# A graph, attention and expert kernel on one core: variance batches, fillers and three small steps in another order

## The chip, the cores and the metric

The kernel runs on one core of a Trainium2 chip. The metric is the device time of one execution in microseconds (us), all work included. The engines are named as in the profile: PE is TensorE's matrix product, PEld its weight load, ACT is ScalarE, DVE is VectorE, POOL is GpSimd, SP is SyncE, which issues the transfers.

## The reference

Three parts follow each other. First a graph network over 50 joints of 4096 frames: three layers of attention over a chain of joints (each joint sees itself and its two neighbours), each with a layer norm over the features and a GELU.

```python
h = _gat(x, src, dst, W, a_s, a_d, bg)      # softmax over neighbours, 4 heads
res = x @ R
x = jax.nn.gelu(_layer_norm(h + res, g, b), approximate=False)
...
x = x.reshape(Bb * Tt, J * DIMS[-1]) @ fpW + fpb
x = _layer_norm(x, fng, fnb)
```

The widths are 3, 64, 128 and 64. The result, one token of 128 numbers per frame, is set beside a text of 128 tokens. Then comes a memory attention (query projection, a causal convolution over 4 steps, a normalised query through two small matrices) and a mixture of 8 experts of width 512, of which each token takes the two best:

```python
h = jnp.concatenate([h, txt], axis=1)
h = h + _L0_attn_ref(_layernorm(h, axis=-1), ...)
h = h + _L0_ffn_ref(_layernorm(h, axis=-1), ...)
```

## The kernel before

The work goes in 16 rounds (`STEPS`). A round takes 256 frames, as two groups of 128 (`GH = 2`), through the three graph layers, and in the gaps it does the attention and the experts of the round before. Everything stays in SBUF, only the inputs of a round, its text and its output move by DMA. Each engine has its own program, written out by hand as one function per step (`window`, `iteration`, `graph_layer` and so on under `block.tensor`, `block.scalar`, `block.vector`, `block.gpsimd`, `block.sync`), and it runs in exactly that order; the engines meet through counting semaphores.

*Tasks.* The joints are taken in chunks of four (13 chunks, the last with two joints). Layer 1 has 26 tasks (chunk and group), layer 2 has 13 (both groups side by side), layer 0 has 14 tasks of its own shape (`task0`, the last two with 128 columns, the others with 512). A task holds up to 512 columns, one PSUM bank.

*Layer 0* (in `window`). PE computes a task's own product (`own_0`, L780) into one of four banks. ACT copies it to SBUF (`take_0`, L1393) and squares every odd task from the bank (L1397); POOL squares the even ones from the copy (`squares_0`, L551). The squares lie in a ring of six (`SQ`, `SQN = 6`), and PE sums them over the features in batches of four tasks (`variance`, L768). A product waits until its bank is free, that is for ACT's copy (even tasks) or square (odd tasks) of the task four before. A square of task 6 or later waits until the batch that read its place in the ring is done. Between them PE runs fillers (`keep_warm`, L684): products of constants whose result nobody reads. Behind the last batch ACT copies the sums (`variance_out`, L1402), PE turns them (`variance_rows`, L788), DVE computes the inverse deviation (`rstd`, from L2112 on, `rsqrt` L2034 to L2041, and its split into bf16 parts L2117 to L2120), PE turns it back (`rstd_rows`, L795), ACT copies it (L1407), PE spreads it over the partitions (`spread_rstd`, L808 and L812) and DVE multiplies (`normalise`, L2138).

*Layers 1 and 2* (`graph_layer` on PE and ACT, `neighbours` on DVE). For each task PE spreads the attention weights (L923, L926), computes the neighbour's product (L906, L909), which ACT copies (`take_d`), and the own product (L944, L948). DVE in layer 2 forms differences of joints (`joint_differences`, L2064 to L2076), scales both neighbours in one operation (L2099), then adds the own product and the neighbour ahead (L2106). POOL subtracts the neighbour behind:

```python
TT(dst, dst, TQ[:, k % 3, 0:cols], ALU.subtract).then_inc(zs_ok, 1)   # take_behind, L580
```

ACT squares the result (`square`, L1484), and PE sums the squares in batches of four tasks; layer 1 has seven batches, layer 2 has four. At the end of a layer PE also starts an expert of the round before: `up(s - 1, e, (0,))` and `(1,)` are two of the four units of an expert's first product (L1043), `down` its second product (L1052). They stand around the last two batches:

```python
if tail:
    pe.wait_ge(d_sb, s * AGG + T0[l] - NT0 + NT[l])
    up(s - 1, e, (0,))
variance(s, l, BATCHES[l] - 2)
if tail:
    pe.wait_ge(t_ok, s * AGG + T0[l] - NT0 + NT[l] + 1)
    up(s - 1, e, (1,))
variance(s, l, BATCHES[l] - 1)
```

The wait for `t_ok` is one for DVE's last scaling, whose banks the unit reuses. ACT's activation of the first unit (`hidden`, L1539) waits for the batch before the last, since it overwrites a place of the ring, and stands ahead of the last square.

*DVE beside the layers.* Behind layer 1's tasks stands the choice of each token's two experts (`top_two`, L2244 to L2270), then `rstd`. Ahead of layer 2's tasks stand the additions of experts (`add_expert`, L2281) and the two sums of the next round's softmax of layer 0 (`alphas(..., (0,))`, L1826 and L1829); its other parts (L1835, L1837) stand behind tasks 2, 5 and 8. Behind layer 2's tasks stand the coordinates of the next round (`coordinates`, from L1885 on), then `rstd`.

Of the kernel before, what the change touches and what calls it, by code (L numbers as in the profile page):

```python
# [10 lines left out]
P = 128  # L11
# [52 lines left out]
def build(nc, A, out):  # L64
# [3 lines left out]
    with ctx:  # L68
# [417 lines left out]
        def _(pool):  # L486
# [87 lines left out]
            def take_behind(s, l, n):  # L574

                c, gh = task(l, n)
                k, cols, o = T0[l] - NT0 + n, joints(c) * P, c * NCOL
                pool.wait_ge(zt_ok, s * AGG + k + 1)
                dst = X2[:, gh, o:o + cols] if l == 1 else X1[:, o:o + cols]
                TT(dst, dst, TQ[:, k % 3, 0:cols], ALU.subtract).then_inc(zs_ok, 1)  # L580

            def layer_1(s):

                mean_differences(s, 1)
                pool.wait_ge(parts_ok, s * 2 + 1)
                pool.wait_ge(x_ok, s * NPAIR + PAIRS[0])
                difference_1(s, 0)
                difference_1(s, 1)
                for n in range(NT[1]):
                    if n % GH == 0 and n // GH + 2 < NCH:  # L590
                        difference_1(s, n // GH + 2)
                    take_behind(s, 1, n)

            def query_pads(s):

# [9 lines left out]
            def iteration(s, nxt):  # L605
                layer_1(s)
                if nxt:
                    pool.wait_ge(r_ps, s * NPAIR + P0[1] + 1)
                    scores_0(s + 1)
                    edges_0(s + 1)  # L610
                mean_differences(s, 2)
                for n in range(NT[2]):
                    take_behind(s, 2, n)
                    if nxt and n == 9:
                        pose_pads(s + 1)
                query_pads(s)
                if nxt:
                    squares_0(s + 1)
# [26 lines left out]
        def _(pe):  # L645
# [338 lines left out]
            def graph_layer(s, l, tail, moe):  # L984

                e = 0 if l == 1 else 4
                if l == 1:
                    product_d(s, l, 0)
                alphas_ready(s, l)
                for n in range(NT[l]):  # L990
                    if l == 2 and n == 1 and tail:
                        added(s - 1, 3)
                    early = l == 2 and n > 0
                    if early and n + 1 < NT[l]:
                        product_d(s, l, n + 1)
                    spread_alpha(s, l, n)
                    if not early and n + 1 < NT[l]:
                        product_d(s, l, n + 1)
                    if n == 0:
                        mean_rows(s, l)  # L1000
                        if l == 1 and moe:
                            added(s - 2, 7)
                    own(s, l, n, True)
                    minus_mean(s, l, n)
                    if l == 1 and n == 5 and tail:
                        token_columns(s - 1, bank[5])
                    if l == 1 and n == 7 and tail:
                        token_logits(s - 1)
                    if l == 1 and n == 9 and tail:
                        pe.wait_ge(lgm_ok, s)  # L1010
                        variance(s, l, 0)
                    elif n % 4 == 3 and n >= 7 and not (n == 7 and l == 1 and tail):
                        variance(s, l, n // 4 - 1)
                if tail:
                    pe.wait_ge(d_sb, s * AGG + T0[l] - NT0 + NT[l])
                    up(s - 1, e, (0,))
                variance(s, l, BATCHES[l] - 2)
                if tail:
                    pe.wait_ge(t_ok, s * AGG + T0[l] - NT0 + NT[l] + 1)
                    up(s - 1, e, (1,))  # L1020
                variance(s, l, BATCHES[l] - 1)
                if tail:
                    pe.wait_ge(hid_sb, (s - 1) * E * MT + e * MT + 2)
# [13 lines left out]
            def up(t, e, units=range(MT)):  # L1037

                for m in units:
                    k = e * MT + m  # L1040
                    if m >= 2 or e == 7:
                        pe.wait_ge(hid_sb, t * E * MT + k)
                    mm(hidden_bank(e, m), w1[:, k * P:k * P + P], XT2[:], start=True, stop=True).then_inc(hid_ps, 1)  # L1043
# [41 lines left out]
            def window(w, main, tail, moe):  # L1085

                t = w - 1
                if main:
                    pe.wait_ge(yt_sb, w * 4 + 4)
                    for n in range(NT0):  # L1090
                        if n == 2 and tail:
                            pe.wait_ge(hf_ok, t + 1)
                        own_0(w, n)
                        if n in (3, 7):
                            keep_warm(3, bank[0])
                        if n % 4 == 1 and n >= 5:
                            keep_warm(2 if n == 5 else 5, bank[0])
                            variance(w, 0, n // 4 - 1)
                    variance(w, 0, BATCHES[0] - 1)
                    if moe:  # L1100
                        up(t - 1, 5, (0,))
                    variance_rows(w, 0)
# [604 lines left out]
        def _(dve):  # L1707
# [371 lines left out]
            def neighbours(s, l, n):  # L2079
# [20 lines left out]
                if l == 2 and n + 1 < NT[l]:  # L2100
# [5 lines left out]
                STT(dst, bZ[(NT0 + k) % 2][:, 0:cols], bgc[:, l - 1:l], TQ[:, 3, 0:cols], ALU.add, ALU.add)\  # L2106
                    .then_inc(zt_ok, 1)

            def rstd(s, l):

                dve.wait_ge(vt_ps, s * 3 + l + 1)
                link(TS(VB.rearrange("p (q a n) -> p q a n", q=CJ, a=4),  # L2112
                        bank[0].rearrange("p (q a n) -> p q a n", q=CJ, a=4)[:, :, :, 0:VR // 4], EPS, None, ALU.add))
                rsqrt(RV, VB, RN)

                vp, rp = (x.rearrange("p (q n) -> p q n", q=CJ) for x in (VB, RV))
                link(nc.vector.tensor_copy(RG[:, :, 0, :], rp))  # L2117
                link(TT(vp, rp, RG[:, :, 0, :], ALU.subtract))
                link(nc.vector.tensor_copy(RG[:, :, 1, :], vp))
                TT(RG[:, :, 2, :], vp, RG[:, :, 1, :], ALU.subtract).then_inc(rg_ok, 1)  # L2120
                dve.wait_ge(zs_ok, s * TASKS + T0[l] + NT[l])
# [221 lines left out]
            def iteration(s, moe, nxt):  # L2343

                t = s - 1
                for n in range(NT[1]):
                    neighbours(s, 1, n)
                    if moe and n == 7:
                        logits(t)
                if moe:  # L2350
                    for part in range(6):
                        top_two(t, part)
# [15 lines left out]
                if moe:  # L2368
                    add_bias(t)
                    add_expert(t, 2)  # L2370
                    add_expert(t, 3)
                if nxt:
                    alphas(s + 1, 0, F0b, M0, Al0, (0,))
                for n in range(NT[2]):
                    neighbours(s, 2, n)
                    if nxt and n in (2, 5, 8):
                        alphas(s + 1, 0, F0b, M0, Al0, ({2: 3, 5: 4, 8: 2}[n],))
                if nxt:
                    coordinates(s + 1, 0)
                rstd(s, 2)  # L2380
# [162 lines left out]
```

## Time and profile before

| what | value |
|---|---|
| median of 3 runs | 4307.02 us (4305.0 to 4308.09) |
| the profiled execution, own time | 4305.8 us |
| its span, first to last instruction | 4304.0 us |
| PE busy | 3816.6 us (89%) |
| DVE busy | 3451.0 us (80%) |
| ACT busy | 2351.6 us (55%) |
| POOL busy | 1507.9 us (35%) |
| granted clock of TensorE, mean | 0.974 of full |
| HBM read and written | 14.72 MB and 4.19 MB |

How to read it: all rows of the trace come from one execution, so a sum over them is set against 4305.8 us. The shares of busy time are means over stages with different limits. The granted clock is 1.00 at 2.4 GHz and 0.50 at 1.2 GHz; a stretch between these had some of each. In a timeline a row may merge several instructions of one kind; the arrow in brackets names who ended an idle time. A product of fp32 operands shows as two instructions in the trace.

### The profile page before, as it was taken

How to read it: one execution, taken by the hardware profiler on the slowest of the kernel's cores; microseconds unless marked ns; L12 is line 12 of the kernel's file. 1: busy time of each engine (PE TensorE's matmuls, PEld its weight loads, DVE VectorE, ACT ScalarE, POOL GpSimd, SP SyncE). 2: the span in 40 equal slices, each digit the busy share in tenths (PEclk: the TensorE clock that was granted, in tenths of full speed). 3: DMA queues.
4: the chain of work that ended last, by engine and by line, in shares of the span. 5: the costliest groups of instructions: out<-in, count | busy, mean ns of one | idle time of the engine just before them, and what ended most of it. 6: DMA issues, size and time to landing. Idle time of an engine off the chain costs nothing.

```text
span 4304.0 us, 61949 instructions
## 1 busy us (share of the span) xinstructions
PE 3816.6 (89%) x22762; PEld 1767.0 (41%) x22762; DVE 3451.0 (80%) x6559; ACT 2351.6 (55%) x3833; POOL 1507.9 (35%) x1513
## 2 busy tenths in 40 slices
PE   4888889898988989889898989989899898988988
PEld 2232344334434344353433434343354343434345
DVE  3878878788787888878788787888878788787872
ACT  2545556465655646556465665646556455664643
POOL 2624315252342524315243341624315243242410
PEclk8898999999999999999999999999999999999999
DMA  2000000000000000000000000000000000000000
GB/s 96 1 4 1 1 6 1 4 3 2 5 1 4 3 4 3 1 6 1 4 3 2 5 1 4 3 4 3 1 6 1 4 3 2 5 1 4 4 2 6
DMA packets 22816, 22.97 MB, mean 5 GB/s; under 512 B 3378, under 2 KB 21818, under 8 KB 22122
## 3 DMA queue, kind: packets, MB, share of 16 engines
q1 hardware_dynamic: 22506, 18.93, 1.4%
q8 instruction: 183, 3.00, 0.3%
q14 instruction: 127, 1.04, 0.1%
HBM read 14.72 MB, written 4.19 MB: 4 GB/s over the span
## 4 chain that ended last, share of the span: by engine, by line
PE 46%; DVE 35%; ACT 10%; issue 7%; POOL 1%; DVEq 0%; SPq 0%; DMA 0%; ACTq 0%; POOLq 0%
DVE R L2099 8%; PE bank L906 7%; PE bank L1043 6%; PE bank L1052 5%; PE bank L768 4%; DVE X L2106 4%; PE bank L840 3%; ACT X L1413 2%; DVE X L2138 2%; DVE R L1831 2%; PE bank L780 2%; PE bank L923 2%; PE bank L909 2%; PE bank L829 2%; DVE R L2073 2%
## 5 line engine op out<-in xcount | busy, mean ns | idle before, releaser
L580 POOL TENSOR_TENSOR X<-X,R 128x512 f32<-128x512 f32 (+1 forms) x624 | 787.4, 1262 | 819.8 <-DVE X L2106 815.8
L2099 DVE TENSOR_TENSOR R<-bank,R 128x1024 f32<-128x1024 f32 (+1 forms) x624 | 738.8, 1184 | 74.5 <-PE bank L923 2.1
L2138 DVE TENSOR_TENSOR X<-X,bank 128x1024 f32<-128x1024 f32 (+2 forms) x432 | 484.7, 1138 | 250.6 <-PE bank L808 125.1
L1413 ACT ACTIVATE X<-X,c_vec 128x1024 f32<-128x1024 f32 (+2 forms) x432 | 498.2, 1173 | 218.3 <-DVE X L2138 215.2
L1043 PE MATMUL bank<-XT,c_w 128*128 128x512 f32 x1024 | 524.1, 627 | 15.4 <-DVE Ho L2281 7.8
L1052 PEld LDWEIGHTS bank<-c_w,SQ 128*128 128x128 f32 x4096 | 489.2, 192 | 90.8 <-issue 84.0
L1052 PE MATMUL bank<-c_w,SQ 128*128 128x128 f32 x4096 | 513.0, 278 | 0.0
L906 PE MATMUL bank<-R,c_W 64*128 64x512 f32 (+1 forms) x832 | 464.7, 639 | 34.1 <-ACT R L1456 18.8
L2106 DVE SCALAR_TENSOR_TENSOR X<-bank,bgc,R 128x512 f32<-128x512 f32 (+1 forms) x624 | 455.9, 731 | 28.4 <-PE bank L960 6.2
L1539 ACT ACTIVATE SQ<-bank,c_vec 128x512 f32<-128x512 f32 x512 | 346.4, 686 | 225.6 <-PE bank L1043 175.2
L944 PE MATMUL bank<-X,WR 64*128 64x512 f32 (+1 forms) x832 | 463.7, 638 | 2.8 <-DVE Ho L2281 2.8
L1454 ACT ACTIVATE R<-bank 128x512 f32<-128x512 f32 (+1 forms) x416 | 241.3, 580 | 376.2 <-PE bank L906 290.5
L1484 ACT ACTIVATE SQ<-X 128x512 f32<-128x512 f32 (+1 forms) x624 | 375.2, 609 | 108.7 <-POOL X L580 102.3
L560 POOL TENSOR_TENSOR Al<-R 128x208 f32<-128x208 f32 x128 | 87.2, 710 | 916.1 <-ACT R L1380 916.1
L1461 ACT ACTIVATE R<-bank 128x512 f32<-128x512 f32 (+1 forms) x208 | 121.4, 584 | 377.9 <-PE bank L910 320.7
L569 POOL TENSOR_TENSOR R<-X 128x512 f32<-128x512 f32 (+1 forms) x208 | 268.2, 1292 | 151.2 <-DVE Pt L1846 95.0
L551 POOL TENSOR_TENSOR SQ<-X 128x512 f32<-128x512 f32 (+1 forms) x112 | 106.6, 952 | 578.8 <-ACT X L1393 577.1
L1043 PEld LDWEIGHTS bank<-XT,c_w 128*128 128x128 f32 x1024 | 176.3, 193 | 256.5 <-issue 129.4
L948 PE MATMUL bank<-X,WR 128*64 128x512 f32 (+1 forms) x832 | 215.0, 594 | 52.5 <-DVE X L2106 50.7
L923 PE MATMUL bank<-AT,sel1b 120*128 120x512 bf16 (+1 forms) x832 | 250.2, 383 | 8.4 <-DVE R L2099 6.7
L910 PE MATMUL bank<-X,c_W 128*64 128x512 f32 (+1 forms) x416 | 217.0, 603 | 0.0
L909 PE MATMUL bank<-X,c_W 128*64 128x512 f32 (+1 forms) x416 | 217.0, 603 | 0.0
(288 smaller groups left out, 6250.0 us busy)
## 6 DMA issues: line engine op xcount, KB each, us to landing
c_w<-in_w SPq DMA_DIRECT2D x2, 2048.0 KB
out<-Ho SPq DMA_DIRECT2D x32, 128.0 KB, 1.9
c_fpW<-in_fpW SPq DMA_DIRECT2D x1, 3200.0 KB
X<-in_x SPq DMA_DIRECT2D x34, 75.0 KB, 2.0
X<-in_txt SPq DMA_DIRECT2D x32, 64.0 KB, 1.9
X<-in_sel SPq DMA_DIRECT2D x1, 600.0 KB
X<-in_sel SPq DMA_DIRECT2D x1, 300.0 KB
X<-in_raw SPq DMA_DIRECT2D x1, 256.0 KB
```

Source lines behind the costliest of these rows:

```text
L580: TT(dst, dst, TQ[:, k % 3, 0:cols], ALU.subtract).then_inc(zs_ok, 1)
L906: mm(bD[:, 0:cols], W1[64 * gh:64 * gh + 64, :], DX[64 * gh:64 * gh + 64, c % 2, 0:cols], start=True, stop=True).then_inc(d_ps, 1)
L923: last = mm(b[:, 0:cols], sel1[:, c % JS, :], AT[:, sign, gh, o:o + cols], start=True, stop=True)
L944: mm(z[:, 0:cols], WR1[64 * gh:64 * gh + 64, :], X1[64 * gh:64 * gh + 64, o:o + cols], start=True, stop=False)
L1043: mm(hidden_bank(e, m), w1[:, k * P:k * P + P], XT2[:], start=True, stop=True).then_inc(hid_ps, 1)
L1052: last = mm(b[:, q * P:q * P + P], HD[:, m, q * P:q * P + P], w2[:, k * P:k * P + P], start=(m == 0 and q == 0), stop=(m == MT - 1), skip_ ...
L1413: A_(dst, dst, ACT.Gelu, bias=v(f"b{l}"), scale=v(f"g{l}")).then_inc(x_ok, 1)
L1484: A_(SQ[:, n % SQN, 0:cols], z, ACT.Square).then_inc(sq_ok, 1)
L1539: A_(HD[:, m, :], hidden_bank(e, m), ACT.Gelu, bias=vec[:, FB1 + k:FB1 + k + 1]).then_inc(hid_sb, 1)
L2099: TT(TQ[:, k % 3:4:3 - k % 3, 0:cols], bR[k % 2][:, :, 0:cols], both, ALU.mult).then_inc(t_ok, 1)
L2106: STT(dst, bZ[(NT0 + k) % 2][:, 0:cols], bgc[:, l - 1:l], TQ[:, 3, 0:cols], ALU.add, ALU.add)\
L2138: TT(dst, dst, b, ALU.mult).then_inc(u_ok, 1)
```

## The change

In every place it is the order that changes, and in one the engine.

- Layer 0 in `window` on PE: the variance batch of tasks 0 to 3 now follows product 7 (before: product 5), that of 4 to 7 follows product 11 (before: 9), that of 8 to 11 follows product 13 as before, and that of the last two tasks is last. Of fillers there are four behind product 3, three ahead of each of the last two batches: ten. Before there were 3, 2, 3, 5 and 5: eighteen.
- The subtraction of the last chunk (`take_behind`) moves from POOL to DVE: two tasks of 256 columns in layer 1, one in layer 2. DVE waits there for POOL's subtraction of the task before.
- In layer 2 the expert unit `up(s - 1, e, (1,))` and its wait stand ahead of the third variance batch.
- On DVE the two sums `alphas(s + 1, 0, ..., (0,))` stand behind task 0 of layer 2 instead of ahead of it.

```diff
@@ gpsimd, layer_1
-                    take_behind(s, 1, n)
+                    if n // GH + 1 < NCH:
+                        take_behind(s, 1, n)
@@ gpsimd, iteration
-                for n in range(NT[2]):
+                for n in range(NT[2] - 1):
                     take_behind(s, 2, n)
@@ tensor, graph_layer
-                variance(s, l, BATCHES[l] - 2)
+                if l == 1:
+                    variance(s, l, BATCHES[l] - 2)
                 if tail:
                     pe.wait_ge(t_ok, s * AGG + T0[l] - NT0 + NT[l] + 1)
                     up(s - 1, e, (1,))
+                if l == 2:
+                    variance(s, l, BATCHES[l] - 2)
                 variance(s, l, BATCHES[l] - 1)
@@ tensor, window
                         own_0(w, n)
-                        if n in (3, 7):
-                            keep_warm(3, bank[0])
-                        if n % 4 == 1 and n >= 5:
-                            keep_warm(2 if n == 5 else 5, bank[0])
+                        if n == 3:
+                            keep_warm(4, bank[0])
+                        if n % 4 == 3 and n >= 7:
                             variance(w, 0, n // 4 - 1)
-                    variance(w, 0, BATCHES[0] - 1)
+                    for i in range(NT0 // 4 - 1, BATCHES[0]):
+                        keep_warm(3, bank[0])
+                        variance(w, 0, i)
@@ vector
+            def take_behind(s, l, n):
+
+                c, gh = task(l, n)
+                k, cols, o = T0[l] - NT0 + n, joints(c) * P, c * NCOL
+                dve.wait_ge(zt_ok, s * AGG + k + 1)
+                dve.wait_ge(zs_ok, s * TASKS + NT0 + k)
+                dst = X2[:, gh, o:o + cols] if l == 1 else X1[:, o:o + cols]
+                TT(dst, dst, TQ[:, k % 3, 0:cols], ALU.subtract).then_inc(zs_ok, 1)
@@ vector, iteration
                     if moe and n == 7:
                         logits(t)
+                take_behind(s, 1, NT[1] - 2)
+                take_behind(s, 1, NT[1] - 1)
...
-                if nxt:
-                    alphas(s + 1, 0, F0b, M0, Al0, (0,))
                 for n in range(NT[2]):
                     neighbours(s, 2, n)
+                    if nxt and n == 0:
+                        alphas(s + 1, 0, F0b, M0, Al0, (0,))
                     if nxt and n in (2, 5, 8):
                         alphas(s + 1, 0, F0b, M0, Al0, ({2: 3, 5: 4, 8: 2}[n],))
+                take_behind(s, 2, NT[2] - 1)
```

The instructions of PE in layer 0 of a round in the middle, before (L780 own products, L684 fillers, L768 variance batches; a count is in instructions of the program):

```order
L780 MATMUL bank<-X,W0bd 128x512 x4
L684 MATMUL bank<-sel1b 128x512 x3
L780 MATMUL bank<-X,W0bd 128x512 x2
L684 MATMUL bank<-sel1b 128x512 x2
L768 MATMUL bank<-SQ,V2p 32x512 x4
L780 MATMUL bank<-X,W0bd 128x512 x2
L684 MATMUL bank<-sel1b 128x512 x3
L780 MATMUL bank<-X,W0bd 128x512 x2
L684 MATMUL bank<-sel1b 128x512 x5
L768 MATMUL bank<-SQ,V2p 32x512 x4
```

The same place in the changed kernel, where the three kinds are L781, L685 and L769:

```order
L781 MATMUL bank<-X,W0bd 128x512 x4
L685 MATMUL bank<-sel1b 128x512 x4
L781 MATMUL bank<-X,W0bd 128x512 x4
L769 MATMUL bank<-SQ,V2p 32x512 x4
L781 MATMUL bank<-X,W0bd 128x512 x4
L769 MATMUL bank<-SQ,V2p 32x512 x4
L781 MATMUL bank<-X,W0bd 128x128 x2
L685 MATMUL bank<-sel1b 128x512 x3
L769 MATMUL bank<-SQ,V2p 32x512 x4
L685 MATMUL bank<-sel1b 128x512 x3
L769 MATMUL bank<-SQ,V2p 32x128 x2
```

Four products now stand in a row ahead of each of the first two batches, and no filler is between them.

The instructions of DVE at the start of layer 2, before (L1826 and L1829 are the two sums, L2099 the scaling, L2106 the addition of a task):

```order
L2281 SCALAR_TENSOR_TENSOR Ho<-bank,router,Ho 128x128 x8
L1826 TENSOR_TENSOR X<-X 128x416
L1829 TENSOR_TENSOR X<-X 128x416
L2064 MEMSET R 128x128
L2073 TENSOR_TENSOR R<-R 128x512
L2099 TENSOR_TENSOR R<-bank,R 128x1024
L2071 TENSOR_TENSOR R<-R 128x128
L2073 TENSOR_TENSOR R<-R 128x512
L2106 SCALAR_TENSOR_TENSOR X<-bank,bgc,R 128x512
L2099 TENSOR_TENSOR R<-bank,R 128x2x512
```

And in the changed kernel (the sums are L1831 and L1834, the scaling is L2104, the addition L2111):

```order
L2295 SCALAR_TENSOR_TENSOR Ho<-bank,router,Ho 128x128 x8
L2069 MEMSET R 128x128
L2078 TENSOR_TENSOR R<-R 128x512
L2104 TENSOR_TENSOR R<-bank,R 128x1024
L2076 TENSOR_TENSOR R<-R 128x128
L2078 TENSOR_TENSOR R<-R 128x512
L2111 SCALAR_TENSOR_TENSOR X<-bank,bgc,R 128x512
L1831 TENSOR_TENSOR X<-X 128x416
L1834 TENSOR_TENSOR X<-X 128x416
L2104 TENSOR_TENSOR R<-bank,R 128x2x512
```

The two sums have moved from ahead of the first differences to between the addition of task 0 and the scaling of task 1.

## Rows read from the trace of the kernel before

**Rows 1.** The page, its first line.

```profile
span 4304.0 us, 61949 instructions
```

**Rows 2.** Timeline, layer 0 (start us, us, engine, line, operation, count, idle before).

```profile
2125.17 0.82 PE L684 MATMUL bank<-sel1b 120*128 120x512 bf16 x3
...
2126.28 1.11 ACT L1393 ACTIVATE X<-bank 128x512 f32<-128x512 f32 x2
...
2127.24 0.65 ACT L1397 ACTIVATE SQ<-bank 128x512 f32<-128x512 f32 x1
...
2128.07 1.06 PE L768 MATMUL bank<-SQ,V2p 128*32 128x512 f32 x8
...
2128.45 1.06 POOL L551 TENSOR_TENSOR SQ<-X 128x512 f32<-128x512 f32 x1 [0.43 <-ACT X L1393]
...
2129.07 1.13 PE L780 MATMUL bank<-X,W0bd 32*128 32x512 f32 x4
...
2131.94 1.25 PE L684 MATMUL bank<-sel1b 120*128 120x512 bf16 x5
...
2138.24 1.12 PE L1043 MATMUL bank<-XT,c_w 128*128 128x512 f32 x2
```

**Rows 3.** Timeline, start of layer 2 in the same round.

```profile
2048.90 0.58 DVE L1826 TENSOR_TENSOR X<-X 128x416 f32<-128x416 f32 x1
...
2052.85 0.29 DVE L2071 TENSOR_TENSOR R<-R 128x128 f32<-128x128 f32 x1 [0.68 <-ACT R L1461]
...
2053.78 0.75 DVE L2106 SCALAR_TENSOR_TENSOR X<-bank,bgc,R 128x512 f32<-128x512 f32 x1
...
2054.61 1.28 POOL L580 TENSOR_TENSOR X<-X,R 128x512 f32<-128x512 f32 x1 [17.75 <-DVE X L2106]
2054.66 1.23 DVE L2099 TENSOR_TENSOR R<-bank,R 128x1024 f32<-128x1024 f32 x1
```

**Rows 4.** Busy time of DVE by stretch, layer 2's loop (us, busy, clock, DMA).

```profile
2053.80:2091.80 38.00, 35.83 (x50) 1.00 0.02 4
```

**Rows 5.** Timeline, end of layer 2, same round; last the view of L1886 (ns).

```profile
2090.50 2.54 POOL L580 TENSOR_TENSOR X<-X,R 128x512 f32<-128x512 f32 x2 [1.28 <-DVE X L2106]
...
2091.28 0.48 DVE L2106 SCALAR_TENSOR_TENSOR X<-bank,bgc,R 128x256 f32<-128x256 f32 x1
...
2092.38 1.31 DVE L1886 TENSOR_TENSOR X<-Al,dX 128x600 f32<-128x600 f32 x1
...
2092.49 1.45 PE L768 MATMUL bank<-SQ,V2p 128*32 128x512 f32 x8 [2.62 <-ACT SQ L1484]
...
2093.86 2.07 PE L1043 MATMUL bank<-XT,c_w 128*128 128x512 f32 x2
...
2098.27 0.29 DVE L2112 TENSOR_SCALAR R<-bank 128x128 f32<-128x128 f32 x1 [2.30 <-PE bank L788]
...
L1886 DVE TENSOR_TENSOR X<-Al,dX x32: 774/778/1312, 54.0 to 3914.8; 128x600 f32<-128x600 f32 x32
```

**Rows 6.** Timeline, end of layer 2 one round later.

```profile
2349.31 0.48 DVE L2106 SCALAR_TENSOR_TENSOR X<-bank,bgc,R 128x256 f32<-128x256 f32 x1
...
2354.87 0.29 DVE L2112 TENSOR_SCALAR R<-bank 128x128 f32<-128x128 f32 x1 [0.87 <-PE bank L788]
```

**Rows 7.** PE by stretch at ends of layer 2 (us, busy, clock, DMA, GB/s).

```profile
1053.00:1061.00 8.00, 5.92 (x20) 0.79 0.00 0
...
4155.00:4163.00 8.00, 4.95 (x17) 0.79 0.04 10
```

**Rows 8.** Timeline, end of layer 1; last the view of L2246 (ns min/median/max).

```profile
2251.16 0.29 DVE L2112 TENSOR_SCALAR R<-bank 128x128 f32<-128x128 f32 x1
...
2255.22 0.42 PE L795 MATMUL bank<-identb,R 128*96 128x128 bf16 x4 [1.49 <-DVE R L2120]
...
L2246 DVE TENSOR_TENSOR router<-router,den x16: 191/520/523, 437.9 to 4234.7; 128x32 f32<-128x32 f32 x16
```

**Rows 9.** Timeline, a DVE product of two tensors with 256 columns.

```profile
2118.45 0.42 DVE L2138 TENSOR_TENSOR X<-X,bank 128x256 f32<-128x256 f32 x1 [2.02 <-PE bank L812]
```

## The prediction

> **What bounds the kernel now.** I read the page first, then the order of the program, then the timeline of one round of the 16 (2040 to 2300 us), then the granted clock. The span is 4304.0 us [rows 1]; the profiled execution took 4305.8 us, 1.2 us under the median 4307.02 us. No engine is the bound all through, so each edit is priced in its own stage. Four places matter.
>
> *Layer 0's own products.* TensorE (PE) runs in program order: products, fillers, a variance batch. The reader is to see that ScalarE (ACT) waits for PE here: two copies take 1.11 us and a square 0.65 us [rows 2], and they overlap, so that a pair costs some 1.43 us and seven pairs under 10 us, while the stage lasts from 2125.17 (after the first four products) to 2138.24, 13.07 us. VectorE (DVE) is on the path only behind it.
>
> *Layer 2's loop.* DVE is busy 35.83 of 38.00 us [rows 4] over 50 operations; the rest is the short gap between dependent ones. Whatever is added there moves the end. Ahead of it, between the first scaling and 2052.85, DVE waits 0.68 us for ACT [rows 3].
>
> *The end of layer 2.* PE sits idle some 2.6 us before the third variance batch; then its clock falls to the lower level. The batch takes 1.45 us, the expert unit behind it 2.07 us, and DVE starts the inverse deviation at 2098.27, 6.99 us after its last addition began (2091.28) [rows 5]. In a round whose clock stays up that stretch is 5.56 us (2349.31 to 2354.87) [rows 6]. Of 15 rounds with an expert, 11 show a mean clock below 1.00 there, the first and the last of them in [rows 7].
>
> *The end of layer 1.* The router's top-two work on DVE ends just when the transposed variances are there: L2112 starts at 2251.16 with no wait shown [rows 8]. It has no slack, and PE waits for DVE behind it.
>
> **The change part by part.** Times are of the same round; 26.14 stands for 2126.14 in layer 0, 91.3 for 2091.3 in layer 2.
>
> *(a) Layer 0: eight fillers fewer, variances later.* A filler costs 0.215 us ((1.25 − 0.82)/2 of 5 and 3), a batch 1.00 us until the next product starts (28.07 to 29.07), a pair of products 1.06 us with what it waits for [rows 2]. Walking the new order: four fillers 25.17 to 26.03, product 4 at 26.14; 5 waits for the square of 1, behind which ACT's copies start at 26.28, so 26.4; 6 starts at 26.87 behind the copy of 2, 7 at 27.94 behind the square of 3 (27.24 + 0.65); batch 0 at 29.0, 8 to 10 at 30.0, 11 at 30.8 behind the square of 7, batch 1 at 31.86, the two small products at 32.86, three fillers to 33.85. Batch 2 waits for GpSimd's (POOL's) square of task 10 (1.06 us, [rows 2]) until 34.3; three fillers, batch 3 to about 36.3. Before: 38.24. That is 1.9 us a round. Bounds: eight fillers alone are 1.7 us; ACT's pace allows 3. Behind it lies a chain of PE, ACT and DVE that starts with the variances, so all of it counts: 16 x 1.9 = **−30 us**.
>
> *(b) Expert unit ahead of layer 2's third batch.* Unit 1 moves into PE's idle stretch: it needs only DVE's last scaling, done when the last addition starts (91.28), so it runs from 91.3 to 92.4, and the gap of 2.6 us becomes one of 1.4. If that keeps the clock, a round saves what the two kinds differ by, 6.99 − 5.56 = 1.43 us, in 11 rounds. In every round it saves little more: behind batch 2 ACT still has an expert activation and the last square, and batch 3 waits for them anyway; some 0.2 us. 11 x 1.43 + 15 x 0.2 = **−19 us**. Bounds: −3 (the clock falls all the same) and −25 (1.65 us in all 15).
>
> *(c) The last subtractions on DVE.* One of 256 columns costs about 0.42 us [rows 9]. In layer 2 it is hidden: POOL's own one (part of 2.54 us) goes, and with it the delay of the next product of the coordinates, 1.31 us instead of the usual 0.78 [rows 5]; DVE stays ahead of the variances: nothing. In layer 1 two of them (0.87 us with their waits) stand ahead of the top-two work, which has no slack. A part comes back: L2246 takes 0.52 us in the median and 0.19 alone [rows 8], since POOL's subtraction ran beside it, and that is gone: +0.55 us. ACT's squares gain nothing, since the activation between them waits for a batch. 15 x 0.55 = **+8 us**. Bounds 0 and +13.
>
> *(d) Layer 0's two sums for the softmax behind the first task of layer 2.* Before, they ran from 48.90 on, the first for 0.58 us [rows 3], ahead of the loop; without them DVE would have waited longer for ACT's copy at 52.85, so they were free. Now they stand behind the addition of task 0 (53.78 + 0.75 [rows 3]) in the saturated loop. Alone the two cost 1.2 us and a short gap, less what they overlap with the addition's end and the wait that they fill: +1.05 us. But POOL starts its subtraction of that task at 54.61 [rows 3]. At the end of layer 2 the same meeting is seen: L1886, second of two DVE multiplications of two SBUF tensors with a POOL subtraction pending, takes 1.31 for 0.78 us [rows 5]; POOL went in between the two. Here POOL would take its 1.1 to 1.3 us between the two sums: the second ends at about 56.6 and the next scaling moves from 54.66 to 56.66, +2.0 us. Bounds +1.05 and +2.2; I take 2.0, since L1886 is the same situation. 15 x 2.0 = **+30 us**.
>
> The Trainium skill speaks against this edit: "SBUF — State Buffer", section "Who interferes with whom", says that a DVE instruction with two SBUF inputs and a GpSimd instruction that reads SBUF lock each other out for a whole instruction. By it the second sum waits for all of POOL's subtraction, the upper end; the trace agrees where it shows it (1.31 against 0.78 us).
>
> *(e) The clock in new gaps.* With (c) PE's gap at the end of layer 1 grows from 1.49 [rows 8] to 2.0 us, with two expert steps of 2 us behind it that would run at half clock. Gaps of 2.6 us behind thin work gave a fall in 11 of 15 rounds; I count a fall here in 6 of 15, at 1.4 us (the price at layer 2): +8. For (a), where PE now runs some 3 us with small products only, and for what is left at layer 2, another +5. Sum **+13 us**; bounds 0 and +35.
>
> Sum: −30 − 19 + 8 + 30 + 13 = +2, against the execution's own 4305.8 us 4307.8 us, and with the 1.2 us between it and the median 4309 us. A measurement of this kernel can tell about 0.2% (8.6 us) from no change, so this is "no change".
>
> **The rivals.**
> 1. *The clock holds everywhere.* (e) is nothing: 4309 − 13 = 4296 us, faster. For it: gaps of 1.5 us at layer 1 never cost the clock. Against it: the gaps grow towards what did.
> 2. *The two sums are cheap.* POOL does not get in between: (d) is 1.05 x 15 = 16 instead of 30: 4295 us, faster. With rival 1 as well: 4282 us. Against it: L1886.
> 3. *The clock falls in more places* (slower): at layer 1's end in every round. Nine more falls of 1.4 us give 4322 us. It decides if the 2.0 us gap works as the 2.6 us one did; its price is the expert steps behind the gap. For it: all gaps of 2.6 us but four fell.
> 4. *The moved expert unit does not keep the clock* (the change does not do there what it is for): (b) is −3 instead of −19: 4325 us. Against it: the gap nearly halves, and the unit fills its end.
>
> **How the numbers follow.** Forecast 0.42, with its own range 4299 to 4315. Rivals 1 and 2 together 0.30, rival 3 0.17, rival 4 0.11. The time is the likeliest case's, 4309 us. The range reaches into rivals 1 and 2 (4287) and over 3 and 4 (4327), which leaves out the double cases. Faster by over 0.2% (under 4298.4 us) 0.30, within it 0.42, slower (over 4315.6) 0.28.
>
> **What would show each step.** (a) ACT's last copy of layer 0 followed by the expert product 1.9 us earlier relative to the first fillers, granted clock 1.00 in the stage. (b) The stretch from DVE's last addition to L2112's successor at about 5.4 us in all rounds, the unit in front of the batch. (c) The same stretch in layer 1 up by 0.5 us, the router's product at 0.19 us. (d) The second sum at over 1 us with POOL's subtraction inside it, and the next scaling 2 us later than before, relative to the first. (e) Falls of the clock behind layer 1's end in about 6 rounds. The prediction is wrong if (d) costs 1 us or less or if layer 0 saves under 1.5 us, and if the falls are fewer than 3 or more than 12.

## The result and the profile after

The changed kernel takes 4312.70 us in the median of 20 runs (4305.62 to 4317.94), the kernel before 4304.74 us in 20 runs of the same series (4296.97 to 4310.08): a ratio of 1.0020 with the interval 1.0013 to 1.0027. The forecast was 4309 us, 2 us over the kernel before; the measured difference is 8.0 us. The sign is measurable, the size stands right at the 0.2% that the prediction called no change.

The page of the changed kernel, its first two lines and the granted clock, against [rows 1]:

```profile
span 4307.5 us, 61756 instructions
...
PE 3799.3 (88%) x22634; PEld 1769.5 (41%) x22634; DVE 3487.7 (81%) x6607; ACT 2349.2 (55%) x3833; POOL 1465.4 (34%) x1465
...
PEclk8999999999999999999999999999999999999999
```

The profiled execution took 4309.3 us, 3.4 us under the median. Its span is 3.5 us longer than before's. The page shows nothing else, since the edits cancel each other. To see them, each round is cut on DVE's timeline at the points that bound its stages, from the start of one pose token (the step that closes a round) to the start of the next. The table gives means over the 15 full rounds in us, and the difference times 15. It is worked out from the timelines of both kernels. A stretch begins and ends where the operations named in it start; the inverse deviation starts at L2112 (L2126 in the changed kernel).

| stretch, from and to | before | after | x15 |
|---|---|---|---|
| pose token to layer 0's inverse deviation | 16.27 | 14.49 | −26.7 |
| first normalised product of layer 0 to first addition of layer 1 (the attention stage) | 45.57 | 45.06 | −7.7 |
| layer 1: last addition to inverse deviation | 4.64 | 5.05 | +6.2 |
| layer 1: inverse deviation to first normalised product | 6.87 | 7.74 | +13.1 |
| layer 2: first addition to next scaling | 0.89 | 2.73 | +27.6 |
| layer 2: last addition to inverse deviation | 6.52 | 5.62 | −13.6 |
| layer 2: inverse deviation to first normalised product | 6.16 | 6.81 | +9.7 |
| the others | 171.27 | 171.21 | −0.9 |
| whole round (sum) | 258.19 | 258.71 | +7.7 |

Ahead of the first pose token 4.3 us are won (313.20 to 308.86 us), which with the +7.7 makes the 3.5 us of the span. In these 4.3 lie the first pass of layer 0, 1.9 us shorter (its inverse deviation starts at 80.03 us for 81.93), and the first pair of sums, 2.0 us longer; the other 4.4 us go with a mean granted clock of 0.88 there for 0.86.

**Layer 0.** The timeline of PE in the changed kernel, for [rows 2] (start us, us, engine, line, operation, operands, count, idle before; L781 own products, L685 fillers, L769 variance batches):

```profile
2124.93 1.04 PE L685 MATMUL bank<-sel1b 120*128 120x512 bf16 x4
...
2125.90 2.92 PE L781 MATMUL bank<-X,W0bd 32*128 32x512 f32 x8
2128.74 1.06 PE L769 MATMUL bank<-SQ,V2p 128*32 128x512 f32 x8
...
2133.10 0.82 PE L685 MATMUL bank<-sel1b 120*128 120x512 bf16 x3
...
2134.14 1.07 PE L769 MATMUL bank<-SQ,V2p 128*32 128x512 f32 x8 [0.21 <-POOL SQ L551]
...
2136.23 1.12 PE L1047 MATMUL bank<-XT,c_w 128*128 128x512 f32 x2
```

From the first of the fillers to the expert product behind the last batch it is 11.30 us; before 13.07 [rows 2]. Batch 2 waits for POOL's square, as the walk said.

**Start of layer 2.** The timeline, for [rows 3]:

```profile
2052.18 0.75 DVE L2111 SCALAR_TENSOR_TENSOR X<-bank,bgc,R 128x512 f32<-128x512 f32 x1
...
2052.85 0.58 DVE L1831 TENSOR_TENSOR X<-X 128x416 f32<-128x416 f32 x1
2053.01 1.55 POOL L580 TENSOR_TENSOR X<-X,R 128x512 f32<-128x512 f32 x1 [17.76 <-DVE X L2111]
2053.47 1.54 DVE L1834 TENSOR_TENSOR X<-X 128x416 f32<-128x416 f32 x1
2055.05 1.23 DVE L2104 TENSOR_TENSOR R<-bank,R 128x1024 f32<-128x1024 f32 x1
```

The scaling starts 2.87 us after the addition, for 0.88 [rows 3]. POOL's subtraction is ready in the middle of the first sum, and goes in ahead of the second, which lasts 1.54 us. It does so in all 15 places behind task 0; the 16th stands ahead of the first round and takes 0.59 us, so that the view by line gives a mean of 1.48 us (busy us, mean ns):

```profile
L1834 DVE TENSOR_TENSOR X<-X 128x416 f32<-128x416 f32 x16 | 23.7, 1484 | 0.6
```

**End of layer 2.** The timeline, for [rows 5]:

```profile
2091.66 0.48 DVE L2111 SCALAR_TENSOR_TENSOR X<-bank,bgc,R 128x256 f32<-128x256 f32 x1
2091.68 1.12 PE L1047 MATMUL bank<-XT,c_w 128*128 128x512 f32 x2 [1.44 <-DVE R L2104]
...
2092.26 0.43 DVE L2121 TENSOR_TENSOR X<-X,R 128x256 f32<-128x256 f32 x1
2092.87 1.06 PE L769 MATMUL bank<-SQ,V2p 128*32 128x512 f32 x8
...
2095.10 0.62 PE L769 MATMUL bank<-SQ,V2p 128*32 128x256 f32 x2 [1.16 <-ACT SQ L1489]
2096.49 0.86 PE L789 MATMUL bank<-c_ident,R 128*128 128x128 f32 x4 [0.78 <-ACT R L1407]
...
2097.15 3.38 PE L1047 MATMUL bank<-XT,c_w 128*128 128x512 f32 x4
2097.46 0.29 DVE L2126 TENSOR_SCALAR R<-bank 128x128 f32<-128x128 f32 x1 [1.10 <-PE bank L789]
...
2102.15 0.39 PE L796 MATMUL bank<-identb,R 128*96 128x128 bf16 x4
...
2104.15 1.22 DVE L2152 TENSOR_TENSOR X<-X,bank 128x1024 f32<-128x1024 f32 x1 [2.67 <-PE bank L813]
```

The batch is at full clock now (1.06 us, for 1.45 [rows 5]) and L2126 starts 5.80 us after the last addition, for 6.99. But the clock falls all the same, some 3 us later: the transposes take 0.86 us and the expert product behind them 3.38 us, so that the transposes of the deviations (L796) come late. Part of what was won is given back. The same two in the kernel before, in the round whose clock holds [rows 6]:

```profile
2354.13 0.63 PE L788 MATMUL bank<-c_ident,R 128*128 128x128 f32 x4 [0.78 <-ACT R L1402]
2354.60 1.88 PE L1043 MATMUL bank<-XT,c_w 128*128 128x512 f32 x4
```

**End of layer 1.** First a round whose clock stays up, for [rows 8]:

```profile
2247.08 0.19 DVE L2260 TENSOR_TENSOR router<-router,den 128x32 f32<-128x32 f32 x1
...
2250.44 0.28 DVE L2126 TENSOR_SCALAR R<-bank 128x128 f32<-128x128 f32 x1
...
2254.50 0.42 PE L796 MATMUL bank<-identb,R 128*96 128x128 bf16 x4 [1.87 <-DVE R L2134]
2254.76 2.00 PE L1056 MATMUL bank<-c_w,SQ 128*128 128x128 f32 x16
...
2257.31 2.35 DVE L2152 TENSOR_TENSOR X<-X,bank 128x1024 f32<-128x1024 f32 x2 [2.86 <-PE bank L809]
```

And the same place in another round of the same execution:

```profile
1474.97 0.42 PE L796 MATMUL bank<-identb,R 128*96 128x128 bf16 x4 [1.87 <-DVE R L2134]
1475.23 3.46 PE L1056 MATMUL bank<-c_w,SQ 128*128 128x128 f32 x16
...
1479.41 2.35 DVE L2152 TENSOR_TENSOR X<-X,bank 128x1024 f32<-128x1024 f32 x2 [4.49 <-PE bank L809]
```

PE's stretches around it (from and to, length, busy, granted clock):

```profile
1471.00:1476.00 5.00, 3.13 (x20) 0.95 0.00 0
1476.00:1480.00 4.00, 4.00 (x21) 0.63 0.00 0
```

The gap of PE is 1.87 us (before 1.49 [rows 8]); in both rounds it is the same. In the second the unit behind it runs at the lower level, 3.46 us for 2.00, and DVE gets its bank 1.64 us later (8.50 for 6.87 us in the table's stretch). That happens in 8 of 15 rounds; before in none.

### The profile page after: what moved, and what is told of

It reads as the page before. It is cut to its first block, busy times and chain, and to the rows that moved or that the text cites. A ratio compares the mean times of both kernels' runs of the same rounds, so it can differ in the third digit from the quotient of the medians.

```text
span 4307.5 us, 61756 instructions
## 1 busy us (share of the span) xinstructions
PE 3799.3 (88%) x22634; PEld 1769.5 (41%) x22634; DVE 3487.7 (81%) x6607; ACT 2349.2 (55%) x3833; POOL 1465.4 (34%) x1465
## 4 chain that ended last, share of the span: by engine, by line
DVE 48%; PE 35%; ACT 9%; issue 6%; POOL 1%; DVEq 1%; SPq 0%; DMA 0%; ACTq 0%; POOLq 0%
DVE R L2104 14%; DVE X L2111 8%; PE bank L1056 6%; PE bank L1047 6%; PE bank L841 3%; PE bank L907 2%; PE bank L781 2%; ACT X L1418 2%; PE bank L769 2%; DVE X L2152 2%; DVE R L1836 2%; DVE R L2078 2%; DVE Ho L2295 2%; PE bank L830 2%; ACT AT L1440 1%
## 5 line engine op out<-in xcount | busy, mean ns | idle before, releaser
L580 POOL TENSOR_TENSOR X<-X,R 128x512 f32<-128x512 f32 x576 | 750.3, 1303 | 829.7 <-DVE X L2111 828.2
L2104 DVE TENSOR_TENSOR R<-bank,R 128x1024 f32<-128x1024 f32 (+1 forms) x624 | 738.7, 1184 | 72.2 <-PE bank L924 1.0
L1047 PE MATMUL bank<-XT,c_w 128*128 128x512 f32 x1024 | 533.4, 638 | 37.1 <-DVE R L2104 21.6
L1056 PEld LDWEIGHTS bank<-c_w,SQ 128*128 128x128 f32 x4096 | 503.2, 196 | 97.5 <-issue 90.7
L1056 PE MATMUL bank<-c_w,SQ 128*128 128x128 f32 x4096 | 525.9, 282 | 0.0
L2111 DVE SCALAR_TENSOR_TENSOR X<-bank,bgc,R 128x512 f32<-128x512 f32 (+1 forms) x624 | 455.9, 731 | 24.5 <-PE bank L961 2.0
L1047 PEld LDWEIGHTS bank<-XT,c_w 128*128 128x128 f32 x1024 | 178.9, 195 | 282.8 <-issue 121.6
```

Of the source, the lines that this page charges most:

```text
L1056: last = mm(b[:, q * P:q * P + P], HD[:, m, q * P:q * P + P], w2[:, k * P:k * P + P], start=(m == 0 and q == 0), stop=(m == MT - 1), skip_ ...
L2104: TT(TQ[:, k % 3:4:3 - k % 3, 0:cols], bR[k % 2][:, :, 0:cols], both, ALU.mult).then_inc(t_ok, 1)
```

## The experiments

Two theories stood against each other. **Sum of the parts:** each edit does what its term says, so that each alone gives its term, and leaving out the costly one gives the rest. **The clock decides:** the parts are right by themselves, but each also shifts where PE's clock falls, so that the parts don't add. Each run's kernel before ran beside it on the same chip (4307.14, 4306.47 and 4306.83 us in three series). Stage times and counts of falls below are of each one's profiled execution, cut as in the table: one execution a kernel, so how they vary between executions was not seen.

**1. Only layer 0's order** (the hunk `@@ tensor, window` of the change alone):

```diff
-                        if n % 4 == 1 and n >= 5:
-                            keep_warm(2 if n == 5 else 5, bank[0])
...
+                        if n % 4 == 3 and n >= 7:
                             variance(w, 0, n // 4 - 1)
...
```

> Layer 0's order alone (four products ahead of a batch, ten fillers), all else as before. Theory A (each term stands by itself): layer 0's stage is 1.8 us a round shorter and everything behind it moves along, 16 rounds, so 27 to 30 us faster than before (ratio 0.993 to 0.994), with the granted clock never falling in that stage. Rival (the gain is given back later, at the attention or the clock): under 15 us faster (ratio above 0.9965).

Measured: 4271.85 us, ratio 0.9920 (0.9907 to 0.9934), so −35, 5 us more than theory A's range. Layer 0 gives 1.78 us a round, −26.7, and 1.9 us in its first pass. Beyond it the attention stage lost 9.6 us of falls and the start 8.3 us (the 1.9 among them), and the end of layer 2 got 10.4 us longer (in 4 rounds 8.11 us, both halves of the stretch at the lower clock). The term holds; what came on top goes with the clock.

**2. Only the two sums:**

```diff
-                if nxt:
-                    alphas(s + 1, 0, F0b, M0, Al0, (0,))
                 for n in range(NT[2]):
                     neighbours(s, 2, n)
+                    if nxt and n == 0:
+                        alphas(s + 1, 0, F0b, M0, Al0, (0,))
```

> Only the two sums of layer 0's softmax moved behind the first task of layer 2. Theory A: DVE's loop is saturated and GpSimd's subtraction gets in between the two sums, so 2.0 us in each of 15 rounds, 28 to 31 us slower (ratio 1.0065 to 1.007). Rival: a part is absorbed by the wait ahead of layer 2's second task, 1.05 us or less a round, at most 16 us slower (ratio 1.004 or less).

Measured: 4338.93 us, ratio 1.0072 (1.0058 to 1.0086), so +32. The next scaling is 1.98 us later in every round whose sums stand there. With layer 0's, this term is what both theories share, and it holds.

**3. The whole change, with the sums back in their old place:**

```diff
+                if nxt:
+                    alphas(s + 1, 0, F0b, M0, Al0, (0,))
                 for n in range(NT[2]):
                     neighbours(s, 2, n)
-                    if nxt and n == 0:
-                        alphas(s + 1, 0, F0b, M0, Al0, (0,))
```

> The changed kernel with the two sums back ahead of the loop (so layer 0's order, the subtractions on DVE and the expert unit). Theory A: the changed kernel less 28 us, so about 4285 us and 20 us faster than before (ratio 0.995). Rival (the parts hide each other): less than 15 us below the changed kernel.

Measured: 4266.99 us, ratio 0.9912 (0.9898 to 0.9925); 46 us under the changed kernel where the sums cost 28. The rest is clock: at the end of layer 1 one fall is left of eight, though the gaps there are alike (1.85 to 2.24 us in the changed kernel, 1.87 to 2.26 us here), and behind the unit in layer 2 none is left of fourteen. That speaks for the second theory: the same gap gave falls or not by what stood elsewhere in the round.

**4. Only the expert unit ahead of the batch:**

```diff
-                variance(s, l, BATCHES[l] - 2)
+                if l == 1:
+                    variance(s, l, BATCHES[l] - 2)
                 if tail:
                     pe.wait_ge(t_ok, s * AGG + T0[l] - NT0 + NT[l] + 1)
                     up(s - 1, e, (1,))
+                if l == 2:
+                    variance(s, l, BATCHES[l] - 2)
```

> Only the expert unit ahead of layer 2's third variance batch. Theory A (from the trace of the changed kernel: the clock no longer falls ahead of the batch but falls behind it in nearly every round, so the stretch to the inverse deviation is 0.9 us shorter and the next one 0.65 us longer): 2 to 6 us faster than before. Rival (the forecast's term): 15 to 20 us faster, ratio 0.996. From the last addition to the inverse deviation about 5.5 us in every round, from there to the first product with it 6.9 us.

Measured: 4297.39 us, ratio 0.9978 (0.9969 to 0.9987), so −10, between the ranges of the two theories: neither was met. The profiled execution was the fastest of its runs, 4289.97, and its start is 7.7 us shorter than before. The stretch to the inverse deviation falls from 6.52 to 5.58 us in the mean (−14.1), the next grows in 9 rounds, for the 14 of the changed kernel, by 0.42 in the mean (+6.3).

**5. Only the subtractions on DVE:**

```diff
+                take_behind(s, 1, NT[1] - 2)
+                take_behind(s, 1, NT[1] - 1)
...
+                take_behind(s, 2, NT[2] - 1)
```

> Only the last subtractions on DVE (two in layer 1, one in layer 2). Theory A: in layer 1 the stretch from the last addition to the inverse deviation grows by 0.42 us a round, in layer 2 it is hidden; 15 x 0.42, about 6 us slower than before (ratio 1.001 to 1.002), plus a fall of the clock behind layer 1 in rounds whose gap lies badly (1.6 us each, 0 to 8 of them). Rival: the shorter delay of the next instruction pays for it, within 2 us of before.

Measured: 4341.25 us, ratio 1.0083 (1.0070 to 1.0097), so +35 where its direct cost (5.08 for 4.64 us) is 6.6. Theory A was missed by far, and this is the best witness of the second theory. Layer 1's end shows a fall in 11 of 15 rounds (+17.1 us), and layer 2's end costs 11.8 us more than before. In six of the eleven rounds layer 2's stretch to the inverse deviation takes 8.10 us; the timeline of such a round:

```profile
2364.11 0.48 DVE L2107 SCALAR_TENSOR_TENSOR X<-bank,bgc,R 128x256 f32<-128x256 f32 x1
...
2365.31 1.93 PE L769 MATMUL bank<-SQ,V2p 128*32 128x512 f32 x8 [2.62 <-ACT SQ L1485]
...
2367.17 2.08 PE L1044 MATMUL bank<-XT,c_w 128*128 128x512 f32 x2
...
2371.02 1.09 PE L789 MATMUL bank<-c_ident,R 128*128 128x128 f32 x4 [0.78 <-ACT R L1403]
...
2372.21 0.29 DVE L2122 TENSOR_SCALAR R<-bank 128x128 f32<-128x128 f32 x1 [3.41 <-PE bank L789]
```

The gap of 2.62 us is that of the kernel before, and the batch behind it at the lower clock from its start, 1.93 us: the whole chain to L2122 then is, and takes 8.10 us instead of 6.99 or 5.56 [rows 5, 6].

**6. The sums split, the first behind task 0, the second behind task 1:**

```diff
-                    link(TT(Mx[:], Mx[:], Fb[:, 2, :], ALU.add))
+                    if 5 not in parts:
+                        link(TT(Mx[:], Mx[:], Fb[:, 2, :], ALU.add))
+                if 6 in parts:
+                    link(TT(Mx[:], Mx[:], Fb[:, 2, :], ALU.add))
...
+                    if nxt and n < 2:
+                        alphas(s + 1, 0, F0b, M0, Al0, ((0, 5) if n == 0 else (6,)))
```

> The kernel before with the two sums in the loop, but one behind task 0 and the other behind task 1 of layer 2, so that GpSimd's subtraction can't stand between them. Theory A (2.0 us a round were 1.05 of length and 0.95 of GpSimd's turn on the way to SBUF): from the first addition to the next scaling 0.45 to 0.6 us longer than before, the same behind task 1, together 1.0 to 1.2 us a round, 15 to 18 us slower than before (ratio 1.0035 to 1.0042). Rival (length and saturation alone, GpSimd plays no part): 2.0 us a round as with both sums together, 28 to 31 us slower (ratio 1.007).

Measured: 4316.11 us, ratio 1.0027 (1.0017 to 1.0037), so +10. The timeline behind task 0:

```profile
2054.34 0.75 DVE L2109 SCALAR_TENSOR_TENSOR X<-bank,bgc,R 128x512 f32<-128x512 f32 x1
2055.01 0.58 DVE L1826 TENSOR_TENSOR X<-X 128x416 f32<-128x416 f32 x1
2055.17 1.56 POOL L580 TENSOR_TENSOR X<-X,R 128x512 f32<-128x512 f32 x1 [17.76 <-DVE X L2109]
2055.63 1.22 DVE L2102 TENSOR_TENSOR R<-bank,R 128x1024 f32<-128x1024 f32 x1
```

With one sum there, the scaling (one operand from the bank, one from SBUF) runs straight through POOL's subtraction, 1.29 us after the addition. Each of the two sums costs 0.40 us, together 0.80 instead of 1.98. Of the difference, 0.95 us is what the second sum of the pair lasted over its own 0.59: the wait for POOL. The time stays under theory A's range of 15 to 18 us. The old place still is better, being free.

**7. The changed kernel with six fillers ahead of layer 1's gap:**

```diff
                     down(t, 0, (0,))
+                    keep_warm(6, bank[3])
```

> The changed kernel with six fillers in TensorE's gap at the end of layer 1, behind the first unit of the expert's second product. Theory A (8 of 15 rounds lost 1.64 us there to the lower clock): the stretch from layer 1's inverse deviation to its first product is 6.87 us in every round again, about 13 us under the changed kernel, 4300 us. Rival (the fillers themselves delay the turned rows): 6.87 us is not reached, or under 5 us gained.

Measured: 4293.63 us, ratio 0.9974 (0.9964 to 0.9984); 19 us under the changed kernel. PE's timeline there:

```profile
2243.35 1.05 PE L1056 MATMUL bank<-c_w,SQ 128*128 128x128 f32 x8
2244.24 1.46 PE L685 MATMUL bank<-sel1b 120*128 120x512 bf16 x6
2246.29 0.42 PE L796 MATMUL bank<-identb,R 128*96 128x128 bf16 x4 [0.58 <-DVE R L2135]
2246.55 2.00 PE L1056 MATMUL bank<-c_w,SQ 128*128 128x128 f32 x16
```

The gap is 0.58 us, L1056 takes 2.00 us, and the stretch is 6.87 us in all 15 rounds: with the gap mostly filled no fall is left at layer 1's end, where they cost 13.1 us. Seven of the fourteen falls in layer 2 went with them, untouched by the fillers.

**8. Layer 0's order and the unit, subtractions and sums as before** (against the changed kernel):

```diff
-                take_behind(s, 1, NT[1] - 2)
-                take_behind(s, 1, NT[1] - 1)
...
+                if nxt:
+                    alphas(s + 1, 0, F0b, M0, Al0, (0,))
```

> Layer 0's order and the expert unit, with the subtractions on GpSimd and the sums ahead of the loop as before. Theory A: the subtractions cost 6 us in the run with the sums back (4267 us), so about 4261 us, 46 us faster than before (ratio 0.989). Rival (what these runs gained beyond their terms was the clock's luck with the length of a round): no faster than 4267 us, for rounds of another length meet more falls.

Measured: 4257.85 us (4256.55 to 4258.93), ratio 0.9889 (0.9874 to 0.9904): 49 us under the kernel before, 55 under the changed one. It beats both. Falls are left in layer 0 (3 rounds, 16.2 for 14.5 us), one at layer 2's end, and 10 in the attention stage of the 14 later rounds (45.7 us and more for 44.8).

**9. Number 8 without the ten fillers of layer 0:**

```diff
-                        if n == 3:
-                            keep_warm(4, bank[0])
...
-                        keep_warm(3, bank[0])
```

> The best so far (layer 0's new order and the expert unit, 4258 us) without any of the ten fillers in layer 0. Theory A (the fillers are there for the clock): TensorE's clock falls in layer 0's stage in half of the rounds or more, the stage from the pose token to the inverse deviation is 16 us or longer there instead of 14.5, and the time is 4265 to 4285 us. Rival (the waits for ScalarE and GpSimd set the pace, the clock holds): the stage is 0.5 to 1 us shorter in every round, 4243 to 4252 us.

Measured: 4315.04 us, ratio 1.0020 (1.0011 to 1.0029), 57 us over number 8 and over what was expected. Layer 0 takes 18.48 us in the mean for 14.83. PE's stretches in one round, the first four products and the rest:

```profile
2129.10:2133.10 4.00, 3.69 (x14) 1.00 0.00 0
2133.10:2147.60 14.50, 13.96 (x52) 0.53 0.00 0
```

and of its timeline:

```profile
2129.16 1.62 PE L780 MATMUL bank<-X,W0bd 32*128 32x512 f32 x8
2131.03 4.52 PE L780 MATMUL bank<-X,W0bd 32*128 32x512 f32 x8 [0.25 <-ACT X L1394]
2135.47 1.94 PE L768 MATMUL bank<-SQ,V2p 128*32 128x512 f32 x8
```

The own products keep PE shown as busy, with no gap over 0.25 us ahead of the fall, and the granted clock still falls to half, in every round. The ten fillers take 2.2 us of PE's time a round (ten of 0.215), and with them the stage is 3.7 us shorter all the same.

**10. The old order of layer 0 with ten fillers (2, 1, 1, 3 and 3), and the unit moved:**

```diff
-                            keep_warm(3, bank[0])
+                            keep_warm(2 if n == 3 else 1, bank[0])
                         if n % 4 == 1 and n >= 5:
-                            keep_warm(2 if n == 5 else 5, bank[0])
+                            keep_warm(1 if n == 5 else 3, bank[0])
```

> The expert unit with layer 0's old order of batches, but with ten fillers (2, 1, 1, 3, 3 in the old places) instead of eighteen. Theory A (the new order is worth something by itself, since in the old one TensorE waits for GpSimd's and ScalarE's squares ahead of the batches): the stage is between 14.9 and 16.0 us, the time 4268 to 4285 us. Rival (only the eight fillers count): the stage is 14.5 us as in the new order and the time 4258 us.

Measured: 4277.06 us (4265.93 to 4285.53), ratio 0.9934 (0.9921 to 0.9948). Layer 0 takes 15.47 us, with no fall: of the 1.78 us that the change gives there, 0.8 come from the eight fillers (eight by 0.215 would be 1.7) and 1.0 from the later batches. Where the fillers are gone, PE waits instead, 1.12 us ahead of the last batches for 0.61 in the kernel before:

```profile
2114.77 1.27 PE L768 MATMUL bank<-SQ,V2p 128*32 128x512 f32 x12 [1.12 <-POOL SQ L551]
```

**11. Number 8 with layer 2's subtraction on DVE, layer 1's on POOL:**

```diff
-                for n in range(NT[2]):
+                for n in range(NT[2] - 1):
                     take_behind(s, 2, n)
...
+                take_behind(s, 2, NT[2] - 1)
```

> The best so far with layer 2's last subtraction, and only that, on DVE. Theory A: it is hidden behind ScalarE's expert activation and TensorE's batch, the stretch from the last addition to the inverse deviation stays at 5.56 us, so 4258 us, within 5 us. Rival: DVE reaches the inverse deviation later, 0.3 us a round or more, 4263 us or above.

Measured: 4257.92 us, ratio 0.9886 (0.9871 to 0.9901), the same as number 8. In layer 2 the subtraction is hidden: the stretch to the inverse deviation is 5.56 us in the mean. The equal time alone would not show it, since falls moved here too: none in layer 0 for three, nine behind layer 2's unit for one. The 9.1 us between numbers 3 and 8 are layer 1's in the main (0.45 us by 15 is 6.8, one fall 1.6).

**12. Number 8 with one filler more, behind product 5:**

```diff
-                        if n == 3:
-                            keep_warm(4, bank[0])
+                        if n in (3, 5):
+                            keep_warm(4 if n == 3 else 1, bank[0])
```

> The best so far with one more filler in layer 0, between products 5 and 6, where TensorE waits for ScalarE's copy. Theory A: the three rounds of fifteen in which the clock fell in that stage (16.2 instead of 14.5 us) go back to 14.5, and the filler fits the wait: 4250 to 4256 us. Rival: the filler delays product 6 and the batch behind it, 0.2 us a round, 4260 us or above.

Measured: 4257.03 us (4255.32 to 4265.71), ratio 0.9882 (0.9867 to 0.9897): no difference from number 8. Layer 0 has no falls here (14.5 us in all rounds), but that is not shown to be the filler's work: number 11 has none either, without it. The profiled execution is the slowest of its runs and has falls behind layer 2's unit in six rounds. Whether its faster runs have them was not seen.

## Why the prediction was right or wrong

*(a) Layer 0, −30:* right. 1.78 us a round in place of 1.9, −26.7 over 15 rounds and −28.6 with the first pass. The walk of the new order holds as well: 11.30 us from the first filler to the expert product for the 11.1 that it gives, with the wait for POOL's square ahead of batch 2. Its bound of 1.7 us for eight fillers alone does not: run 10 gives 0.8, since PE then waits for POOL.

*(b) Expert unit, −19:* the term that failed. The step was "If that keeps the clock, a round saves what the two kinds differ by", 1.43 us. The fall ahead of the batch did go in every round (5.49 to 5.84 us, −13.6), but the clock fell behind the unit instead in 14 of 15 rounds, which costs 0.55 to 0.8 us each time (+9.7). What is left is −3.9, close to the lower bound of −3: rival 4 is what happened, at its own price. The prediction looked as far as the inverse deviation, and the price stood behind it, where L796 waits for a slow L1047.

*(c) Subtractions, +8:* right; 0.42 us for 0.55, +6.2, with L2260 at 0.19 us as said. That layer 2's one is free is shown by run 11.

*(d) The two sums, +30:* right. 1.98 us in each of 15 places is 29.7; the table has 14 of them (+27.6, its last round has none) and the start has one. POOL's turn between the two is the cause: 1.54 us for the second. Run 6, which takes the second away from POOL's turn, confirms it. The sentence of the Trainium skill that the prediction weighed ("SBUF — State Buffer", "Who interferes with whom") stood against this edit, and the trace and run 6 agree with it. Rival 2 is ruled out.

*(e) The clock in new gaps, +13:* at layer 1's end 8 falls of 1.64 us, +13.1, for the 6 of 1.4 that were counted as +8; rival 3, a fall in every round, is ruled out. The +5 for other places came out as −7.7 in the attention stage and −4.4 at the start, beside what (a) and (d) did there. Rival 1, no falls, is ruled out as well.

So three terms hold to within 2 us. Of the rest, (b) was 15 us too hopeful and the price at layer 1's end 5 us too low, while the clock in other places was put 17 us too high. That these met, and the time lies within 4 us of the forecast, is luck: rival 4 put its own mechanism at 4325 us. The rows explain the 3.5 us between the two profiled executions; the other 4.5 us of the measured 8.0 lie between executions that left no rows. The prediction took the clock's falls as a price per gap. The runs show that this is not so: alone, the four edits give −35, +32, −10 and +35, together +22, while all in one kernel give +8. In the changed kernel, every one of the 14 later rounds whose attention stage lasts 45.7 us or more has layer 1's stretch at 6.87, and every one at 44.8 has it at 8.50. That is no rule: in four of those at 44.8 the granted clock was down for 2.7 us in that stage too, where it cost nothing; run 5 has two rounds with 46.44 and 8.4 us, and run 3 one with 47.02 and 8.50. In layer 2 the same gap of 2.62 us goes with 5.56, 6.99 and 8.10 us. What sets in which round the clock falls stays open; only which places it can fall at, and what each costs, was read.

## What to carry to other kernels

Price an edit's own work by its stage and expect that to hold within a few tenths of a microsecond, but don't add up what clock falls cost from runs of single edits: they move from one thin place of a round to the next, so compare the combination. Before DVE operations with two SBUF inputs are put side by side in a saturated loop, look when the GpSimd operation beside them gets ready: here a single one cost 0.40 us, under its length of 0.58, and the second of a pair waited 0.95 us for GpSimd's turn. Where a unit is moved to bridge a gap, follow the path at least to the next wait behind the stage that was mended.

## What was not expected of the hardware

- The granted clock came down to a mean of 0.53 with PE shown busy 3.69 of 4.00 us before and 13.96 of 14.50 us in the fall, with own products of 32 rows and variance products of 32 columns (run 9). The busy share of the profile did not foretell it.
- Gaps of 1.85 to 2.26 us at layer 1's end gave 8 falls in 15 rounds in the changed kernel and 1 in run 3, with the same instructions around it.
- One fall costs 1.64 us at layer 1's end, 1.1 to 1.5 us ahead of layer 2's batch, 2.5 us there when the whole chain is in it, and 0.55 to 0.8 us behind the moved unit.
